# Output projection of a gated attention block: from float32 operands to half-precision parts

## The reference, cut to what matters

```python
# x: (2, 512, 128); context: (2, 32, 128); 16 heads of 64; 8 experts of 256
latents = layernorm(layernorm(x))             # the rows of x are the queries
q = latents @ Wq
k, v = split(concat([ctx_norm @ Wkv, latents @ Wkv]))
attn = softmax(rmsnorm(q) * scale @ rmsnorm(k).T + mask)
out = attn @ v                                # (2, 512, 1024)
x = x + tanh(g_xattn) * (out @ Wout + bout)   # the output projection: Wout is (1024, 128)
h = layernorm(x)
w = top-2 routing of softmax(h @ router)      # over 8 experts
x = x + tanh(g_ffn) * sum_e w_e * (silu(h @ gate_e) * (h @ up_e)) @ down_e
```

## Time and profile before

| | before |
|---|---|
| median of 3 runs | 354.6 us (354.53 to 356.05) |
| the profiled execution: its own time | 354.47 us |
| its span, first to last instruction | 352.7 us |
| PE busy | 305.6 us (87%) |
| DVE busy | 286.0 us (81%) |
| ACT busy | 200.6 us (57%) |
| POOL busy | 256.1 us (73%) |
| mean granted TensorE clock | 0.958 of 2.4 GHz |

### The profile page before, as it was taken

How to read it: one execution, slowest core, us unless ns; L and a number is a source line. 1 busy time by engine, 2 the same in 40 slices (tenths; PEclk the granted TensorE clock), 3 DMA queues, 4 the chain that set the end, 5 groups by cost and what they waited for, 6 DMA issues and landing times.

```text
span 352.7 us, 8708 instructions
## 1 busy us (share of the span) xinstructions
PE 305.6 (87%) x3321; PEld 184.8 (52%) x3321; DVE 286.0 (81%) x553; ACT 200.6 (57%) x340; POOL 256.1 (73%) x193
## 2 busy tenths in 40 slices
PE   0567666899999999999999999999996999779993
PEld 0233223255555555565655557678764656345652
DVE  3887858788899898898998958767658987899994
ACT  2463744577756756766667556567743555335551
POOL 8689965498999998989989978455862354245562
PEclk9996859899999999999999999999999999879998
DMA  6406311830812615408117176430100000001001
GB/s 180 129 1 141 62 24 21 168 83 16 173 43 52 148 33 121 94 16 179 45 27 170 39 207 128 135 122 14 33 4 1 2 1 2 0 1 32 3 0 32
DMA packets 33707, 23.62 MB, mean 67 GB/s; under 512 B 10818, under 2 KB 33154, under 8 KB 33666
## 3 DMA queue, kind: packets, MB, share of 16 engines
q1 hardware_dynamic: 32722, 23.03, 28.2%
q10 hardware_dynamic: 944, 0.04, 0.2%
HBM read 5.87 MB, written 0.52 MB: 18 GB/s over the span
## 4 chain that ended last, share of the span: by engine, by line
PE 57%; POOL 14%; issue 11%; DVE 10%; ACT 4%; DMA 2%; POOLq 0%; SPq 0%; DVEq 0%; ACTq 0%
PE big L1422 8%; PE big L1423 7%; POOL p_lo L588 7%; PE o_ps L1265 5%; PE big L1284 5%; PE o_ps L1259 4%; PE o_ps L1260 4%; PE pj L1236 3%; POOL rms_r L463 3%; PE tv L1272 3%; PE pj L1195 2%; PE tv L1219 2%; PE o_ps L1478 1%; DVE nm_main L908 1%; PE pj L1197 1%
## 5 line engine op out<-in xcount | busy, mean ns | idle before, releaser
L563 POOL TENSOR_TENSOR p_lo<-p 128x1024 f16<-128x1024 f32 x64 | 121.8, 1916 | 12.6 <-ACT p L723 12.6
L908 DVE TENSOR_REDUCE nm_main<-big 128x2 f32<-128x1024 f32 x64 | 78.2, 1222 | 19.8 <-PE big L1284 19.0
L723 ACT ACTIVATE p<-big 128x1024 f32<-128x1024 f32 x64 | 65.6, 1025 | 47.2 <-PE big L1423 47.1
L588 POOL TENSOR_TENSOR p_lo<-p,p_lo 128x512 f16<-128x512 f32 x32 | 37.0, 1158 | 47.4 <-ACT p_lo L795 45.1
L463 POOL TENSOR_TENSOR rms_r<-meansq,power 128x8 f32<-128x8 f32 x32 | 52.3, 1637 | 18.4 <-DVE meansq L882 18.4
L1422 PE MATMUL big<-w 128*128 128x512 f16 x128 | 49.2, 385 | 1.7 <-ACT p L723 1.7
L1423 PE MATMUL big<-w 68*128 68x512 f16 x128 | 48.9, 382 | 0.0
L1259 PE MATMUL o_ps<-v,p 128*128 128x65 f16 x512 | 40.3, 193 | 0.0
L1260 PE MATMUL o_ps<-v,p 128*128 128x64 f16 x512 | 40.2, 194 | 0.0
L1259 PEld LDWEIGHTS o_ps<-v,p 128*128 128x128 bf16 x512 | 35.6, 99 | 6.7 <-issue 3.6
L1260 PEld LDWEIGHTS o_ps<-v,p 128*128 128x128 bf16 x512 | 34.1, 97 | 3.1
(11 more groups left out here) (196 smaller groups left out, 713.6 us busy)
## 6 DMA issues: line engine op xcount, KB each, us to landing
w<-hl SPq DMA_DIRECT2D x32, 256.0 KB, 4.1
w<-hl SPq DMA_DIRECT2D x32, 128.0 KB, 3.7
pc_st<-pc_hi SPq DMA_DIRECT2D x64, 32.0 KB, 1.9
pc_st<-pc_lo SPq DMA_DIRECT2D x32, 32.0 KB, 1.9
hl<-n_kernel_gating_EDF_dram SPq DMA_DIRECT2D x1, 1024.0 KB, 6.0
hl<-L_ffn_kernel_up_EDF_dram SPq DMA_DIRECT2D x1, 1024.0 KB, 5.6
o_sb<-in_L_xattn_Wkv_dram SPq DMA_DIRECT2D x2, 384.0 KB, 6.8
x_sb<-in_x_dram SPq DMA_DIRECT2D x2, 256.0 KB, 3.7
```

The source lines that it names most:

```text
L563: nc.gpsimd.tensor_tensor(p_lo[m % NP][:, :], p[m % NP][:, :], p_hi[m % NP], ALU.subtract).then_inc(plo_ok, 1)
L588: nc.gpsimd.tensor_tensor(hid_lo[m % NH], hid[m % NH], hid_hi[m % NH], ALU.subtract).then_inc(hlo_ok, 1)
L723: nc.scalar.activation(p[n % NP][:, :], st_ps, ACT.Exp).then_inc(exp_ok, 1)
L908: nc.vector.tensor_reduce(nm_main[:, u % 2, 2 * c:2 * c + 2, q], s2_ps.rearrange("p (k n) -> p k n", k=2), AX_X, ALU.max, negate=True).the ...
```

## The change

The turned blocks are kept as two half-precision parts instead of one float32 block, and so are the weights. `evacuate` writes the high half as float16; a new `turned_lo` on VectorE subtracts it from the turned block, still in `tv`, and writes the low half as float16. `project_o` then does three products per block (high x high, high x low weights, low x high weights), 12 matmuls with half-precision operands for a step in place of 4 in float32. The turning of the next block and the projection wait for VectorE's `oTl_ok` instead of ScalarE's `oTa_ok`. `turned_lo` of step i is the last VectorE instruction of slots 49 to 60; in expert slots 2 to 5 it follows the two gating instructions. The weights are no longer loaded at the start: they land in `z` at slot 10, ScalarE makes their high half at slot 26 and GpSimd the low half at slot 28.

```diff
@@ transfers
-            sp.dma_start(wout[:, :, :], Wout.rearrange("(c p) d -> p c d", p=P)).then_inc(rest_in, 16)
+                if n == 10:
+                    sp.wait_ge(zT_ok, 3)
+                    sp.dma_start(wout, Wout.rearrange("(c p) d -> p c d", p=P)).then_inc(rest_in, 16)
@@ GpSimd, slot(n)
+                if n == 28:
+                    pool.wait_ge(wohi_ok, 1)
+                    nc.gpsimd.tensor_tensor(wout_lo[:, :, :], wout, wout_hi[:, :, :], ALU.subtract).then_inc(wolo_ok, 1)
@@ ScalarE
-                nc.scalar.copy(o_half(j), turned_o()).then_inc(oTa_ok, 1)
+                nc.scalar.copy(o_parts(j)[0], turned_o()).then_inc(oTa_ok, 1)
+                if n == 26:
+                    act.wait_ge(rest_in, 16 * 3)
+                    nc.scalar.copy(wout_hi[:, :, :], wout).then_inc(wohi_ok, 1)
@@ VectorE
+            def turned_lo(i):
+                hi, lo = o_parts(O_ORDER[i])
+                dve.wait_ge(oTa_ok, i + 1)
+                nc.vector.tensor_tensor(lo, turned_o(), hi, ALU.subtract).then_inc(oTl_ok, 1)
@@ VectorE, slot(n), behind the low half of the expert weights
+                if n in TURN_AT:
+                    turned_lo(TURN_AT[n])
@@ VectorE, expert_slot(n), behind the two gating instructions
+                if n in TURN_X:
+                    turned_lo(TURN_X[n])
@@ TensorE, project_o(i); turn_o waits for oTl_ok in the same way
-                pe.wait_ge(oTa_ok, i + 1)
+                pe.wait_ge(oTl_ok, i + 1)
-                    last = nc.tensor.matmul(y_bank(t), o_half(j)[:, c * P:(c + 1) * P], wout[:, h * (H // 4) + c, :],
-                                            start=(h == 0 and c == 0 and t <= QT), stop=(h == 1 and c == H // 4 - 1),
-                                            skip_group_check=True)
+                    cols, w = slice(c * P, (c + 1) * P), h * (H // 4) + c
+                    nc.tensor.matmul(y_bank(t), hi[:, cols], wout_hi[:, w, :], start=(h == 0 and c == 0 and t <= QT),
+                                     stop=False, skip_group_check=True)
+                    nc.tensor.matmul(y_bank(t), hi[:, cols], wout_lo[:, w, :], start=False, stop=False, skip_group_check=True)
+                    last = nc.tensor.matmul(y_bank(t), lo[:, cols], wout_hi[:, w, :], start=False,
+                                            stop=(h == 1 and c == H // 4 - 1), skip_group_check=True)
```

More of the change, by code:

```diff
@@ L80, in flamingo_gated_block @@
         wqkv_hi, wqkv_lo = wqkv_hl[:, 0:NG * W3], wqkv_hl[:, NG * W3:2 * NG * W3].bitcast(BF16)
-        wout = sb("wout", [P, H // 2, D], F32)
+        wout_hi = sb("wout_hi", [P, H // 2, D], F16)
+        wout_lo = sb("wout_lo", [P, H // 2, D], BF16)
         wr = sb("wr", [P, E], F32)
@@ L293, in o_half, with o_parts @@
             return o_sb[j // (2 * QT)][:, j // 2 % QT, j % 2 * HALF:(j % 2 + 1) * HALF]
+        def o_parts(j):
+            parts = o_half(j).bitcast(F16)
+            return parts[:, 0:HALF], parts[:, HALF:2 * HALF]
         def y_bank(t):
@@ L1209, in turn_o @@
                 else:
-                    pe.wait_ge(oTa_ok, i)
+                    pe.wait_ge(oTl_ok, i)
                 if i == 2 * QT:
@@ L1485, in slot @@
                 if n == NORM_AT + 2:
-                    pe.wait_ge(oTa_ok, 3 * QT)
+                    pe.wait_ge(oTl_ok, 3 * QT)
                     turn_rows2(0)
@@ L1540, in expert_slot @@
                 if n == ROWS_X:
-                    pe.wait_ge(oTa_ok, 2 * T)
+                    pe.wait_ge(oTl_ok, 2 * T)
                     turn_rows2(1)
```

5 lines of the change are left out of this document (4 added, 1 removed).

## The result

| | before | after |
|---|---|---|
| median (lowest to highest, runs) | 355.33 us (354.53 to 358.73, 4) | 365.03 us (364.76 to 365.65, 4) |
| the profiled execution: its own time | 354.47 us | 364.76 us |
| its span | 352.7 us | 363.0 us |
| mean granted TensorE clock | 0.958 | 0.941 |

The ratio after to before is 1.026, with an interval of 1.019 to 1.033: slower, though the interval leaves open whether by more than 2%. The kernel before has one execution more here, of 358.73 us, than in the table ahead of the prediction. The forecast was 358.8 us, at most 361.8. The direction was right, the size was short by 6 us.

What follows compares the result with a forecast made beforehand. TensorE was taken to bound the projection stage, VectorE's queue expert slots 2 to 7. Attention 1.1, expert 2.8 and weights 0.3 made 4.2 us over 354.47: 358.8 us, range 355.8 to 361.8.

Steps and rivals of the forecast that it cites:

- TensorE's gain: Projection step falls from 0.97 to 0.67 us: 3.6 us in slots 50 to 61, 1.2 us in the expert slots.
- When `turned_lo` is ready: It takes 0.69 us, ending by 1.51 us into slot 54, before the projection wants it at 1.61 us.
- Slots with a residual: Slots 52, 54, 56, 58: residual queued behind turned_lo; projection waits 0.6 us, slot net 0.3 us longer.
- The weighing: Whether the port lock VectorE shares with GpSimd holds turned_lo: one operand in PSUM, so free; otherwise up to 1.89 us each.
- Odd slots: Slots 53, 55, 57, 59: a late weight half delays turned_lo; TensorE waits 0.35 us, eating its 0.30 us gain.
- Slots 52, 53, 56: TensorE's work comes later behind VectorE's delayed division or maxima: +0.2, +0.25 and +0.6 us.
- Expert slots: Four turned_lo in VectorE's full queue, walked through slots 2 to 7; projection 12 stops TensorE 2.3 us; +2.8 us.
- Behind 291 ... I give nothing back: After 291 us, behind expert slots 2 to 7, both engines are near full, so none of the 2.8 us is recovered.
- The weights: Late load costs 0 (up to 0.5), ScalarE's copy 0, GpSimd's low half at slot 28 0.3 us (1.89 at most).
- The sum: Attention slots 1.1, expert slots 2.8, weights 0.3: 4.2 us over the profiled 354.47 us, giving 358.8 us.
- everything late adds up: Rival: weight halves held by GpSimd in some six slots, its inserted work's delay carried on; 361.5 to 364 us; 15 in 100.
- GpSimd insertion: Low half of the weights put into GpSimd's queue at slot 28; in the rival its delay carries on, 1.89 us for 0.3.

Runs made afterwards that it cites:

- experiment 2: Kernel before, float32 projection kept, only VectorE's subtraction added, with turning and projection waiting for it; 367.47 us, ratio 1.032.
- Experiment 3: Changed kernel with the residual's sum left in PSUM, so its second instruction has one operand in SBUF; 361.01 us, ratio 1.014.
- the later execution: A later profiled execution of the same changed kernel, with no edit; span 360.4 us, clock 0.960.
- experiment 5: Changed kernel without turned_lo in the expert slots, steps 12 to 15 in float32 as before; 359.99 us, ratio 1.010.
- experiment 10: The changed kernel run once more, no edit; 364.04 us over 6 runs, ratio 1.024.
- experiment 1: Kernel before, float32 throughout, only the load of the projection weights moved from the start to slot 10; 356.17 us against 356.47, ratio 0.998.
- experiments 8 and 9: New VectorE order, residual sum in PSUM, early weight halves moved: 8, changed kernel, half precision only in attention slots, 352.31 us; 9, kernel before, float32, 353.69 us.
- experiment 4: Changed kernel with the residual ahead of turned_lo in VectorE's queue in slots 50 to 61, expert slots unaltered; 363.64 us, ratio 1.022.

## Why the prediction was right in kind and short in size

**TensorE's gain.** Right: 0.66 us for twelve matmuls against 0.67 forecast. That most of it is lost to waits was right as well; experiment 2 shows it from the other side.

**When `turned_lo` is ready.** Right. It takes 0.69 us beside GpSimd in each of the rows shown above, with its one operand in PSUM, as forecast.

**Slots with a residual.** Here the prediction failed. It had: "That one takes 0.35 or 0.68 us; I take 0.35, since GpSimd only begins its next operation 2.3 us into a slot (230.82)." That is true of slot 54, where I read it: the wait there is 0.47 us, against 0.6. It isn't true of slot 58. There GpSimd has the context low half to make first, and the low half of the probabilities follows it without a gap; at 248.08 it is 1.73 us into TensorE's slot (from 246.35), and L1009 comes at 1.97. The trace of before had shown both things that were missed:

```profile
227.24 1.89 POOL L563 TENSOR_TENSOR p_lo<-p 128x1024 f16<-128x1024 f32 x1 [2.71 <-ACT p L723]
...
242.28 0.38 PE L1422 MATMUL big<-w 128*128 128x512 f16 x1
...
243.72 1.89 POOL L563 TENSOR_TENSOR p_lo<-p 128x1024 f16<-128x1024 f32 x1
```

Slot 58 begins at 242.28, and the low half of the probabilities already came 1.44 us into it, ahead of the 1.8 that I had forecast for L1009. And the 0.68 us of the earlier trace rows, which I put aside, ran from 228.60 to 229.28 beside a GpSimd operation that ended at 229.13: it was the same meeting, with only 0.5 us of GpSimd's operation left. So the residual takes 1.81 us and the wait is 2.15 us in place of 0.6: 1.55 us too little in the sum. Experiment 3 takes the operand out of SBUF and has 0.35 us and a wait of 0.70 us in the same place. The weighing was itself at fault: I asked about `turned_lo` alone, the operation that is added, and not about the operations that it pushes to a later time. L1009 has two operands in SBUF like L1133 of the earlier trace rows, which took 2.40 us, and I gave it no upper end above 0.68 us.

**Odd slots.** Waits of 0.15 and 0.43 us in slots 55 and 59, against 0.35: right on average. In the later execution they are 0.97 and 0.43. (The working gives 0.3 us for a pair of slots; the sum behind it takes 0.4, 0.35 and 0.2 for the three pairs, which comes to nearly the same.)

**Slots 52, 53, 56.** Right: 1.26, 0.50 and 1.59 us of waiting, where the working for slot 56 gives 0.70 + 0.9 = 1.6. What was left out is slot 51: its wait for the transfer of the context low halves was 1.55 us in the first execution, and none in the second. That is no constant cost: of these 1.55 us 0.8 come back in the later execution's slot 55, and the rest is the difference between the two in slots 50 to 62 (3.72 and 2.96).

**Expert slots.** The path was right: projection 12 waited 2.19 us (forecast 2.3), and by experiment 5 the loss is that of the four `turned_lo`. The term was "2.8" from the walk through slots 2 to 7, and with the clock at its full level, in the later execution, slot 7 is another 3.24 us late. What the walk lacked is again L1009, in slot 5: 1.22 us for 0.35 beside GpSimd. In experiment 3, with 0.35, the wait behind it is 1.15 us for 2.02, 0.9 less. That is more than the 0.44 us that the term was short of, so some other part of the walk was too high by about 0.4; which part that is stays open. The first execution had 4.62 us by slot 7, 1.4 more than the later one, for the fall of the clock behind the wait of slot 5. "Behind 291 ... I give nothing back" held for the first (-0.3 us to slot 20); in the later one 0.8 us come in addition between slots 15 and 18, with the fall of the clock shown in experiment 10. The prediction had no term for the clock at all.

**The weights.** Right in place and size: 0.36 against 0.3 us (GpSimd's low half took 2.13 us for 1.89), and experiment 1 has nothing for the load.

**The sum.** Slot by slot, slots 52 to 57 of the first execution cost 1.6 us where the sum had 1.5, but slots 58 and 59 cost 1.96 where it had 0.2, and 1.95 in the later one. Of the 6.1 us that were missing in the first execution, 1.84 are the clock at the start, 1.8 slots 58 and 59 (1.55 of it the residual's wait), 0.7 the transfer in slot 51, and 1.56 the expert stage (its clock behind the wait of slot 5 is 1.4 by slot 7); 0.2 are left. So over half of what was missing in that execution is the clock, which differs between executions. In the later execution only 7.39 - 4.2 = 3.2 us are missing, of which 1.9 are in slots 50 to 62 (nearly all of it slots 58 and 59; that the missing wait of slot 51 and the longer one of slot 55 cancel is luck) and 1.3 in the expert stage (0.8 of it the fall of the clock behind slot 16). The medians say 9.7 us and 8.2 us (364.04 - 355.87), which is 4.0 to 5.5 above the forecast's 4.2. Since both kernels' executions spread (353.0 to 359.5 us before, 362.2 to 365.65 after), what the medians have above 7.39 may be how often the clock fell in the executions met; no run here settles it.

**The rivals.** That everything late adds up (361.5 to 364) was nearest, at 15 in 100, though 365.03 lies outside it and 364.04 at its edge, and not by its GpSimd insertion, which cost 0.36 us. What was added up was one long residual in each stage, and the clock. The range, 361.8 at the top, held neither median.

## What to carry to other kernels

When an instruction is put into a queue, look up for each instruction that it pushes back what the other engines do at its new time, in every slot and not in one that stands for the others. An instruction that is short now can be five times as long (0.35 and 1.81 us) if it comes a quarter of a microsecond after another engine's start instead of before it. A shorter job on the engine that seems the bound is worth something only if the operand comes in time: here the queue's order, with the residual's sum in PSUM, was worth 1.3 to 1.8 us without any half precision (up to 0.5 of it a transfer's wait that comes and goes), and half precision 1.2 to 1.7 us only after it. These are differences of profiled executions; the medians of experiments 8 and 9 alone don't tell them apart. And when two traces are compared, look at the granted clock in each stretch before a difference is put down to the edit: here a fall of the clock cost up to 1.7 us.

## What the runs showed of the hardware

- A result left in PSUM takes an instruction out of the lock: 0.35 against 1.81 us for the same residual at the same place in GpSimd's operation. The hold is then met by the next instruction that has both operands in SBUF (weight half, 0.68 us when free, 1.92 held).
- The instruction that is held need not have two large operands. `ln_v<-moments`, 128x4 with one tensor read, took 1.47 us in experiment 4 (to 246.82) and 1.20 us at 250.70 in the changed kernel (to 251.90). Each time a GpSimd low half ended at about the same moment (246.77, taking half of the two operations' length, and 251.87). At 243.30 in the kernel before it took 0.48 us, and that too ended with a GpSimd operation (at 243.75). I had not expected it to be held at all.
- TensorE's clock at the start differs between executions of the same program (0.50 and 1.00 from 66 to 70 us in the two of the changed kernel). Over all runs, which but for the load of the weights have the same instructions up to slot 9, the differences there to the profiled execution of before were 1.84, 0.64, 2.9, -0.19, 0.62, 0.01, -0.19, 2.09, 2.70, -0.98 and 0.02 us. A comparison of two profiled executions has to begin behind that.
- After TensorE had stood still for 2.02 us in expert slot 5 its clock fell (0.57 over the next 4 us, a gate matmul 0.63 us for 0.38), which costs 1.6 us beyond the wait. The same wait in the same program passed without it in the later execution, and so did the 2.15 us wait of slot 58 in both (1.00 from 250 to 258 us in the first, from 247 to 256 in the later). In experiment 5 it fell behind waits of 1.59 and 2.01 us, in experiment 4 behind waits of 1.87, 2.19 and 2.01 us; the wait of 1.62 us in slot 56 of experiment 4 passed without.
